# Two transformer blocks on one core: fewer maxima ahead of the first score, and VectorE's and GpSimd's other work on other beats

## What is computed

```python
mod = (_silu(L0_c) @ L0_wmod).reshape(8, 6, 1, -1)      # sa, ca, ga, sb, cb, gb
h = _layernorm(x, axis=-1) * (1 + ca) + sa
q, k, v = (einsum('bsd,hdk->bhsk', h, W) + b for W, b in ...)
scores = einsum('bhqk,bhsk->bhqs', q, k) / sqrt(8)       # causal mask
weights = softmax(where(causal_mask, -1e9, scores), axis=-1)
x = x + ga * (einsum('bhqs,bhsk->bhqk', weights, v).reshape(...) @ Wo + bo)
```

## Time and profile before

| | |
|---|---|
| median of 3 runs | 1036.01 us (1034.02 to 1037.21) |
| the profiled execution | 1032.57 us, span 1030.8 us |
| PE busy | 926.3 us (90% of the span) |
| DVE busy | 782.6 us (76%) |
| ACT busy | 749.8 us (73%) |
| POOL busy | 535.5 us (52%) |
| first layer's attention | from about 25 us to 312 us |

### The profile page before, as it was taken

The page is one execution under the profiler, slowest core; times in us unless marked ns, Lnnn a source line. Parts: engine busy times, 40 slices in busy tenths (PEclk is TensorE's granted clock), DMA queues, the critical chain, the costliest instruction groups (busy, mean ns, idle before and its releaser), DMA issues. The chain is left out here.

```text
span 1030.8 us, 23002 instructions
## 1 busy us (share of the span) xinstructions
PE 926.3 (90%) x8664; PEld 512.4 (50%) x8664; DVE 782.6 (76%) x1326; ACT 749.8 (73%) x1380; POOL 535.5 (52%) x748
## 2 busy tenths in 40 slices
PE   5789899889888999999999799899999999889896
PEld 3234343334436888888888533333333333333575
DVE  4778878877855776767877678879798898894476
ACT  2488888778786566676655489788888898889663
POOL 4376766677541111332112078676777868566343
PEclk9699999999999999999999999999999999999998
DMA  7323432222105532335223021111202021100011
GB/s 178 104 73 115 136 94 78 60 76 61 40 26 141 160 92 58 109 94 154 77 78 109 7 84 33 56 37 51 75 14 76 12 87 33 56 14 14 24 32 52
DMA packets 63598, 73.91 MB, mean 72 GB/s; under 512 B 14136, under 2 KB 46008, under 8 KB 63104
## 3 DMA queue, kind: packets, MB, share of 16 engines
q1 hardware_dynamic: 62336, 69.23, 23.5%
q10 hardware_dynamic: 1152, 3.21, 1.0%
HBM read 39.24 MB, written 2.77 MB: 41 GB/s over the span
## 5 line engine op out<-in xcount | busy, mean ns | idle before, releaser
L872 ACT ACTIVATE at_E<-at_Sb 128x512 f32<-128x512 f32 x832 | 442.1, 598 | 78.2 <-PE at_Sb L718 72.4
L944 DVE TENSOR_REDUCE mx<-at_Mb 128x2 f32<-128x1024 f32 x242 | 281.6, 1216 | 41.3 <-PE at_Mb L681 40.1
L718 PE MATMUL at_Sb<-QP,KP 64*128 64x512 bf16 (+3 forms) x1024 | 195.9, 341 | 16.3 <-ACT full_k L419 7.1
L766 PE MATMUL at_Ob<-at_E,VP 128*32 128x256 f32 (+2 forms) x2816 | 204.7, 371 | 1.9 <-POOL at_E L1048 0.6
L1048 POOL TENSOR_TENSOR at_E<-at_E,factor 128x512 f32<-128x512 f32 x128 | 162.4, 1273 | 75.2 <-ACT at_E L872 65.2
L681 PE MATMUL at_Mb<-KP,QP 62*128 62x512 bf16 x996 | 169.4, 348 | 17.3 <-DVE mx L944 16.1
L947 DVE TENSOR_REDUCE mx<-at_Mb 128x2 f32<-128x768 f32 (+1 forms) x128 | 136.7, 1085 | 52.0 <-PE at_Mb L681 51.0
L1059 POOL TENSOR_SCALAR_AFFINE_SELECT at_E<-at_E 128x512 f32<-128x512 f32 x128 | 79.8, 644 | 72.4 <-ACT at_E L872 72.4
L718 PEld LDWEIGHTS at_Sb<-QP,KP 64*128 64x128 bf16 x1024 | 72.9, 95 | 75.6 <-ACT at_E L872 31.4
L681 PEld LDWEIGHTS at_Mb<-KP,QP 62*128 62x128 bf16 x996 | 51.1, 95 | 103.5 <-issue 49.1
L766 PEld LDWEIGHTS at_Ob<-at_E,VP 128*32 128x32 f32 x2816 | 58.3, 108 | 88.6 <-issue 66.6
(11 more groups left out here) (212 smaller groups left out, 1443.0 us busy)
## 6 DMA issues: line engine op xcount, KB each, us to landing
QP<-q SPq DMA_DIRECT2D x96, 128.0 KB, 2.4
KP<-k SPq DMA_DIRECT2D x91, 128.0 KB, 2.4
ex_R<-rw_dram SPq DMA_DIRECT2D x32, 256.0 KB, 3.4
ctxN<-Oev SPq DMA_DIRECT2D x16, 256.0 KB, 2.5
denB<-rdram SPq DMA_DIRECT2D x64, 64.0 KB
ex_R<-rw_dram SPq DMA_DIRECT2D x16, 224.0 KB, 3.7
ex_R<-rw_dram SPq DMA_DIRECT2D x16, 192.0 KB, 3.5
ex_R<-rw_dram SPq DMA_DIRECT2D x16, 160.0 KB, 3.2
```

Source lines behind the costliest of these rows:

```text
L718: return pe.matmul(out[:, at:at + SEQ - q0], KP[p0:p0 + ROWS_H, b % 2, 2 * g + a, kt * P:(kt + 1) * P], QP[p0:p0 + ROWS_H, b % 2, 2 * g + ...
L766: last = pe.matmul(Ob[VW * i:VW * (i + 1), 0, q0:q1], weights_of(b, G, kt, i, q0), moving, start=(kt == 0 and q0 == 0), stop=False, skip_g ...
L872: nc.scalar.activation(dst, src, ACT.Exp).then_inc(s["s_read"], 1)
L944: v.tensor_reduce(mx[:, G % 2, :, t % 2, t // 2], src, AX.X, ALU.max).then_inc(s["m_read"], 1)
```

## The change

The setup asks for x before the conditioning vector, clears VP at its start, normalises batch 0 on VectorE instead of GpSimd, and transposes before the two bias matmuls. In the first layer START becomes -9; in beats 2, 5, 14 and 20 of batch 0 a second maximum is taken at the end of TensorE's beat, so that the lead grows from 9 to 13. The first two groups' shifts are transposed in beats -2 and 4 instead of -4 and 2. The front of batch 1 moves from beats 0, 2 and 5 to 2, 4 and 7, its statistics from beat -4 to 0 and its normalisation from -3 to 1. In the other batches VectorE's statistics go from beat 7 to 4, their aggregation from 8 to 7, the reciprocal from 9 to 8, the context product from 17 to 16, and the weight operations to (4,10), (4,22) and (5,10). GpSimd's power goes from beat 10 to 11, q's split from 19 to 18, and k's split from beat 3 of the next batch to beat 23.

```diff
@@ -130,9 +130,9 @@
         def _(sp):
-            sp.dma_start(cT[:], dram["c"]).then_inc(s["c"], 16)
             sp.dma_start(x[:, 0:SEQ].rearrange("p (t d) -> p t d", t=TILES),
                          dram["x"][0].rearrange("(t p) d -> p t d", p=P)).then_inc(s["x0"], 16)
+            sp.dma_start(cT[:], dram["c"]).then_inc(s["c"], 16)
             sp.dma_start(wmod[:], dram["wmod"]).then_inc(s["wmod"], 16)
@@ -155,9 +155,8 @@
             g.memset(sb["ones"][:], 1.0)
+            g.memset(sb["VP"][:], 0.0).then_inc(s["zero"], 1)
             front_powers(g, sb, front, 0)
-            front_normalise(g, sb, front, 0)
-            g.memset(sb["VP"][:], 0.0).then_inc(s["zero"], 1)
             g.wait_ge(s["zero"], 2)
@@ -200,14 +199,13 @@
+            t.wait_ge(s["ident"], 1)
+            front_transpose(t, sb, front, 0, fb[:, 0, :])
             t.wait_ge(s["columns"], 16)
...
             last.then_inc(s["mm"], 1)
-
-            t.wait_ge(s["ident"], 1)
-            front_transpose(t, sb, front, 0, fb[:, 0, :])
             t.wait_ge(s["scaled"], 1)
@@ -244,6 +242,7 @@
             front_aggregate(v, sb, front, 0)
+            front_normalise(v, sb, front, 0)
             v.wait_ge(s["mm"], 1)
@@ -545,14 +544,15 @@
         BPG = 6 if causal else 8
-        LEAD = 11 if causal else LEAD1
-        START = -LEAD if causal else 0
+        START = -9 if causal else 0
+        DOUBLE_AT = (2, 5, 14, 20) if causal else ()
         BPB = BPG * GROUPS
...
         LN_AT, Q_AT, K_AT, V_AT, RECIP_AT, CTX_AT, OUT_AT = (
-            (14, 17, 20, 6, 9, 17, 19) if causal else (24, 26, 28, 8, 10, 20, 22))
+            (14, 17, 20, 6, 8, 16, 19) if causal else (24, 26, 28, 8, 10, 20, 22))
+        STATS_AT, AGGR_AT, POWERS_AT = (4, 7, 11) if causal else (LN_AT - 7, LN_AT - 6, LN_AT - 4)
         WEIGHTS_AT = 21 if causal else OUT_AT + 3
@@ -565,7 +565,7 @@
-        EARLY = {0: "ln", 2: "q", 5: "k"} if causal else {0: "ln", 3: "q", 6: "k"}
+        EARLY = {2: "ln", 4: "q", 7: "k"} if causal else {0: "ln", 3: "q", 6: "k"}
         FIRST = 2
@@ -581,11 +581,15 @@
+        first_max = 2 if causal else 0
+
         def fills(beat):
...
             out = []
-            if (beat + 4) % BPG == 0 and 0 <= (beat + 4) // BPG < ALLG:
+            if (beat + 4) % BPG == 0 and first_max <= (beat + 4) // BPG < ALLG:
                 out.append(("max", (beat + 4) // BPG))
+            if causal and beat in (-2, 4):
+                out.append(("max", 0 if beat < 0 else 1))
             n, at = divmod(beat, BPB)
@@ -606,23 +610,25 @@
-        def m_of(beat):
-
-            m = beat + LEAD
-            return divmod(m, BPG) if 0 <= m < BPG * ALLG else None
-
-        s_slot, m_slot = {}, {}
+        def ms_of(beat):
+
+            m = beat + (9 if causal else LEAD1) + sum(at < beat for at in DOUBLE_AT)
+            return [divmod(i, BPG) for i in range(m, m + 1 + (beat in DOUBLE_AT)) if 0 <= i < BPG * ALLG]
+
+        s_slot, m_slot, shifts_at = {}, {}, {}
         for name in (("ln", 0), ("q", 0), ("k", 0), ("v", 0)):
...
             s_slot[("max", 0)] = len(s_slot)
-            for m in range(LEAD):
+            for m in range(LEAD1):
                 m_slot[("max",) + divmod(m, BPG)] = m
...
                 s_slot[name] = len(s_slot)
-            if m_of(beat) is not None:
-                m_slot[("max",) + m_of(beat)] = len(m_slot)
+            for m in ms_of(beat):
+                m_slot[("max",) + m] = len(m_slot)
+                if m[1] == BPG - 1:
+                    shifts_at[beat + 1] = m[0]
             if out_of(beat) is not None:
@@ -798,8 +804,8 @@
             for beat in range(START, END):
-                if m_of(beat) is not None:
-                    max_score(*m_of(beat))
+                for m in ms_of(beat)[0:1]:
+                    max_score(*m)
                 if causal and out_of(beat) is not None:
@@ -824,6 +830,8 @@
                     out_proj(out_of(beat))
+                for m in ms_of(beat)[1:]:
+                    max_score(*m)
@@ -960,29 +968,29 @@
             for beat in range(START, END):
-                if m_of(beat) is not None:
-                    reduce_max(*m_of(beat))
+                for m in ms_of(beat):
+                    reduce_max(*m)
                 if out_of(beat) is not None:
...
                 n, at = divmod(beat, BPB)
-                if causal and beat == -4:
+                if causal and beat == 0:
                     v.wait_ge(sb["x1"], 16)
...
                     front_aggregate(v, sb, s, 1)
-                if at == LN_AT - 7 and 2 <= n + 2 <= last_b:
+                if at == STATS_AT and 2 <= n + 2 <= last_b:
                     if causal and n == 0:
...
                     front_stats(v, sb, s, n + 2)
-                if at == LN_AT - 6 and 2 <= n + 2 <= last_b:
+                if at == AGGR_AT and 2 <= n + 2 <= last_b:
                     front_aggregate(v, sb, s, n + 2)
-                if causal and (n, at) == (4, 3):
+                if causal and (n, at) == (4, 10):
                     v.wait_ge(sb["experts_loaded"], 48)
                     v.tensor_scalar(sb["hi"]["w1"][:], sb["w_raw"]["w1"][:], 1.0, None, ALU.mult).then_inc(ex["hi1"], 1)
-                if causal and (n, at) == (4, 15):
+                if causal and (n, at) == (4, 22):
                     v.wait_ge(ex["hi1"], 1)
...
                      .then_inc(ex["lo1"], 1)
-                if causal and (n, at) == (5, 3):
+                if causal and (n, at) == (5, 10):
                     v.wait_ge(ex["hi3"], 1)
@@ -990,7 +998,7 @@
                     expert_normalise(v, sb, ex, 0)
-                if causal and (n, at) == (6, 23):
+                if causal and (n, at) == (6, 22):
                     v.wait_ge(s["s_read"], s_slot[("elog", 0)] + 1)
@@ -1066,10 +1074,9 @@
                 n, at = divmod(beat, BPB)
-                G, off = divmod(beat + LEAD - BPG, BPG)
-                if off == 0 and 0 <= G < ALLG:
-                    shifts(G)
-                if causal and beat == -3:
+                if beat in shifts_at:
+                    shifts(shifts_at[beat])
+                if causal and beat == 1:
                     front_powers(p, sb, s, 1)
@@ -1078,16 +1085,14 @@
                     split(EARLY[beat], 1)
-                if at == LN_AT - 4 and 2 <= n + 2 <= last_b:
+                if at == POWERS_AT and 2 <= n + 2 <= last_b:
                     front_powers(p, sb, s, n + 2)
-                if at == LN_AT - 3 and 2 <= n + 2 <= last_b:
+                if at == (POWERS_AT if causal else LN_AT - 3) and 2 <= n + 2 <= last_b:
                     normalise(n + 2)
-                if at == Q_AT + (2 if causal else 1) and FIRST <= n + 2 <= last_b:
+                if at == Q_AT + 1 and FIRST <= n + 2 <= last_b:
                     split("q", n + 2)
-                if not causal and at == K_AT + 1 and FIRST <= n + 2 <= last_b:
+                if at == K_AT + (3 if causal else 1) and FIRST <= n + 2 <= last_b:
                     split("k", n + 2)
-                if causal and at == 3 and FIRST <= n + 1 <= last_b:
-                    split("k", n + 1)
                 if not causal and (n, at) in ((6, 13), (7, 3)):
```

## The result

The changed kernel takes 1053.62 us (median of 4 runs, 1046.68 to 1055.24), the kernel before 1035.01 us beside it (1031.32 to 1037.21): a ratio of 1.0183, 95% interval 1.0148 to 1.0218. It is 18.6 us slower. The prediction said 1049, with 0.62 on slower. One execution each of experiment 7 (2071 us), experiment 10 (4007 us) and the kernel before (2824 us) was disturbed and is left out of the ratios. The profiled execution is 1055.24 us with a span of 1053.5, so the spans shown here differ by 22.7 us. From 330 us on, where the code is the same, 4.4 of these 22.7 come up. That part takes between 715 and 724 us in the fourteen traces, without a pattern by kernel, so I leave it out.

What follows compares the result with a forecast made beforehand. No engine is full; TensorE is nearest and issues in fixed order, so its every wait is time. 0.1 + 11.1 + 4.2 - 2.8 - 1.0 + 1.5 = +13.1 us on 1036.01 gives 1049, range 1030 to 1057.

Steps and rivals of the forecast that it cites:

- K's split, +11.1: Batches 1 to 6, beat 2: TensorE waits 1.9 us each for GpSimd's third diagonal behind K's split; +11.1 us.
- v projection as a cover: At the split's old place, beat 3, the v projection of beat 6 (1.1 us) covered it; that cover is gone.
- Alignment of the maxima, +4.2: Lead 13: beat 3 to 5 takes 1.82 us, before 1.45; net +0.7 in six batches, +4.2 us.
- Weight operations, -2.8: VectorE's three operations on expert weights, batches 4 and 5: 1.7 us together on short-maxima beats against 4.5; -2.8 us.
- Up to the first beats of batch 1, +0.1: Start up to beat 24: the wait for shift rows swallows the start's gain; +0.1 us.
- 12.3 - 1.1 + 2.4 + 0.4: Batch 0, first score to beat 7: 14.0 us instead of 12.3, so beat 7 at 49.9.
- the wait of 0:12: Batch 0, beat 12: TensorE waits 3.2 us for group 2's shift rows behind K's projection chain; score at 58.5.
- cover themselves: Batch 0, doubled maxima at beats 14 and 20 cost nothing extra: 16.6 us instead of 16.9 to beat 24.
- Tail, -1.0: Last batch: two more beats have no maxima; -1.0 us.
- Clock, +1.5: New idles of 1.9 us can bring the half clock; one such drop, +1.5 us.
- rival *faster: Diagonal and shift rows come in time, the change does what its placement suggests: 1028.5 to 1032.7, say 1031; chance 0.26.
- rival *slower by the clock: Every idle of 1.9 us in the six batches is followed by a half clock stretch: 1058; chance 0.12.

Runs made afterwards that it cites:

- experiment 7: Kernel of experiment 6 with doubled maxima only at 2, 5, 14 (lead 12), VectorE's statistics, aggregation at 5, 8, weight operations a beat later: 1037.27 us, ratio 1.0028.
- experiment 10: Kernel of experiment 7 with batch 1's statistics at beat -2, normalisation at -1 and K projected in beat 5: 1030.47 us, ratio 0.9973.
- experiment 1: Changed kernel with K's split alone put back to beat 3 of the next batch: 1042.98 us, ratio 1.0102.
- experiment 8: Changed kernel with K's split at beat 0 of the next batch, right behind the third diagonal: 1042.65 us, ratio 1.0114.
- Experiment 12: Changed kernel with VectorE's three weight operations put back on beats 4:3, 4:15 and 5:3: 1053.93 us, ratio 1.0213.
- experiment 4: Kernel before with the setup's part of the change alone: 1031.99 us, ratio 0.9991.
- experiment 6: Changed kernel with K's split back at beat 3 and VectorE's reciprocal and context product back at beats 9 and 17: 1043.73 us, ratio 1.0093.
- experiment 2: Kernel before with K's split alone moved from beat 3 of the next batch to beat 23: 1046.51 us, ratio 1.0134.
- experiments 9: Changed kernel with batch 1's statistics at beat -2 instead of 0, power and normalisation at -1 instead of 1: 1053.56 us, ratio 1.0195.
- experiment 11: Kernel before with new setup, START -9, doubled maxima at 2 and 5, batch 1's statistics, normalisation at -2, -1, front at 2, 4, 5: 1029.79 us, ratio 0.9968.
- Experiments 5: Changed kernel with batch 1's K projected in beat 5 instead of beat 7: 1051.80 us, ratio 1.0205.
- experiment 3: Changed kernel with two doubled maxima (beats 2 and 5) instead of four, so lead 11: 1061.97 us, ratio 1.0282.

## Why the prediction was right, and where its steps were off

The forecast was 13.1 us more; 18.6 came (the two medians), inside the range, and by the mechanism that was named as decisive.

- **K's split, +11.1: right.** 10.6 by experiment 1, 11.0 by experiment 8. (By the ratios, each against the kernel before timed beside it, it is 8.4 and 7.1; by the distances of the table 10.55 and 9.4.) I had GpSimd's chain from beat 21 at 8.1 us and a wait of 1.9. The wait at the values is 1.51, and batch 3 is 1.74 longer by the split's place (35.75 less 34.01); batch 1 loses less (0.7) and batch 5 more (3.0), by the weight operation on beat 4:22 and the stretch at 1.2 GHz behind it. What I said of the v projection as a cover is not the point: experiment 8 has the split at beat 0, far in front of that projection, and there the same 3.1 us of GpSimd cost nothing either.
- **Alignment of the maxima, +4.2 (0.7 a batch): right.** Batch 3 takes 34.0 in experiment 1 and 33.2 before, 0.8 more, which is 4.8 in six; the beats 2:3 to 2:5 take 1.83 us (forecast 1.82). In batch 3 three of the groups have 1.83 for 1.45, and in the second group, where the statistics no longer stand, it is 1.83 for 2.11: 0.86 in sum. Experiment 7 removes it with a lead of 12 (and some of VectorE's work a beat later), by 4.8 us. No run has a lead of 13 with everything else on the old beats, but the beats' lengths place most of the 0.8. (Batch 2 takes 34.0 before, not the 33.1 that I read; 33.2 is an ordinary batch like the third.)
- **Weight operations, -2.8: wrong, 0.** The step said that on beats with short maxima the three cost 1.7 instead of 4.5. Experiment 12 finds no difference. Batches 4 and 5 of experiment 4, with the old beats and the old lead, take 3.7 us more than two batches like the third; in experiment 1, with the new ones, 3.6. By the same reckoning the kernel before has 5.2, of which 1.5 are a stretch at 1.2 GHz that experiment 4 lacks at the same operations. So the 4.5 for the old places was too high, and the 1.7 for the new ones too low: they cost 3.6. On top of that comes what the one on beat 4:22 does to GpSimd's diagonal and to the wait of 5:2. I had mentioned that it can block GpSimd, and put that inside the 1.9.
- **The context product, not priced.** I counted one beat earlier for product and reciprocal as nothing. The chain behind it goes over two DMAs, and in batch 2 VectorE waited 2.11 us for it; that was worth some 1.3 us there, and 0.8 in all (experiment 6). Cause and place are shown, the total is near the limit of what can be measured.
- **Up to the first beats of batch 1, +0.1: wrong, +3.2.** The setup came as said (projections 11.69 for 11.4, first maximum 23.45 for 24.1), and so did the first score (34.02 for 34.6). VectorE's second small SiLU step took 0.98 instead of 0.17 us, until GpSimd's clearing of VP ended:

```profile
1.64 3.50 POOL L158 MEMSET VP<- 128x4096 f32 x1
...
4.19 0.98 DVE L241 TENSOR_SCALAR c_silu<-c_silu 128x16 f32<-128x16 f32 x1
```

  The Trainium skill ("SBUF — State Buffer", "SBUF: two separate sides") has this as an exclusive lock of the shared port, and the trace agrees. It changed nothing in the sum, as forecast.

  The loss comes behind the first score, in three places. First, "12.3 - 1.1 + 2.4 + 0.4", the way to beat 7, took 15.2 instead of 14.0. The transposes came at 39.12, even earlier than forecast (41.0 less 1.3). But TensorE stayed at 1.2 GHz until 45.9. In experiment 1, with the same wait for the normalisation, the full clock is back at 43.6, and from the transposes to beat 7 it takes 9.05 us, where I had 8.9 and the changed kernel has 10.1. So this part is the clock, and I had not priced it. The old start does not always do better: 42.5 in the kernel before, but 46.8 in experiment 2, whose code is the same up to there. What is shown is that without the late normalisation the full clock comes early: 40.6 to 41.3 in experiments 9, 10 and 11, and 43.6 to 49.3 in the eight traces with it.

  Second, the wait of 0:12 came where it was forecast but shorter (1.74 instead of 3.2), and the score at 59.59 instead of 58.5; behind it 1.2 GHz came again, 59.5 to 63.0. Third, the doubled maxima at 14 and 20 do not "cover themselves": beats 15 and 21 take 1.22 us each instead of 0.45, the length of one reduction. In experiment 10, which doubles at 14 but not at 20, only beat 15 does, and in experiment 11 neither. From 0:13 to 1:0 it takes 17.9 us where I had 16.6. Experiments 5 and 9 show that each repair of the start falls into the other's wait; with both, 1:1 is at 76.2 and 74.9 (experiments 10 and 11).
- **Tail, -1.0: about 0.** From 7:1 to the end of the attention it is 30.3 in both.
- **Clock, +1.5: one drop as forecast, worth 0.9.** Of the waits for the third diagonal one, that of 1.93 us, was followed by a stretch at 1.2 GHz. Its 0.9 us (an estimate from the lengths of beats 5:2 to 5:5) lie inside the 10.6 above, so they don't count twice. The start's two were not in this term. In all, the first layer ran 34.1 us at 1.2 GHz instead of 23.9.

The two large terms held. The -2.8, the -1.0 and the start's 3.1 are 6.9 us that came out worse; the total is 5.5 above the forecast, mostly because the clock's 1.5 did not come on top.

The rival *faster* fell, and experiment 8 shows why: GpSimd has time enough, but in its fixed order the diagonal was behind the split. The rival *slower by the clock* did not come with the change; it nearly came in experiment 2 (four of six) and in experiment 3 (five of six). Nine maxima ahead of the first score, with the new setup and the early statistics, gain 3 us (experiment 11); what the change has besides cost some 22 (ratios 1.0183 and 0.9968).

## What to carry to other kernels

On an engine with a fixed order, low busy time says nothing about whether a further piece of work is free: ask what stands right behind it and how soon another engine needs that, and put side work directly behind the operation that someone waits for. Look also at what another engine runs at that moment: here one operation of VectorE more than tripled a diagonal of GpSimd (2.24 us for 0.63). Where a ring of two buffers is filled ahead, changing the lead changes which pieces meet the busy beats, so lead, order and places have to be moved together and judged as a set. Where the start is made shorter, follow each chain until the beats where it hides again: two late producers cover for each other, and mending one shows the other.

## What the runs showed of the hardware that I had not expected

The length of an idle stretch of TensorE does not settle by itself whether the granted clock falls behind it. The four waits of 1.51 us in the changed kernel were not followed by 1.2 GHz; its waits of 1.74 and 1.93 were, and so was the one of 1.45 before and in experiment 11. Of six equal waits of 2.11 us in experiment 2 four were followed by it and two were not, and a wait of 2.19 in experiment 11 and one of 2.28 in experiment 3 were not. Four windows of experiment 2, the first two at the full clock:

```profile
81.99:85.00 3.01, 2.60 (x43) 1.46 (x47) 1.77 (x3) 2.32 (x5) 0.85 (x2) 1.00 0.02 4
154.20:157.00 2.80, 2.40 (x39) 1.35 (x39) 1.57 (x2) 2.12 (x5) 0.64 (x2) 1.00 0.04 9
190.10:193.00 2.90, 2.90 (x30) 1.54 (x22) 1.85 (x3) 2.03 (x4) 0.28 (x1) 0.51 0.07 16
118.50:121.50 3.00, 3.00 (x28) 1.28 (x22) 2.85 (x3) 2.58 (x5) 1.22 (x2) 0.50 0.22 72
```

Experiment 4 has the same operations around beat 5:3 as the kernel before, the same wait of 1.45, and no such stretch there. A long wait isn't needed either: in experiment 8 the clock fell at 143.4, where the longest idle time of TensorE in the 5 us before was 0.73 us, and the same instructions with a wait of 0.74 in experiment 1 kept the full clock. This is that stretch of experiment 8 as a window:

```profile
143.40:146.80 3.40, 3.40 (x20) 1.43 (x21) 1.01 (x2) 1.08 (x2) 1.13 (x2) 0.50 0.00 0
```

What tells the cases apart stays open.
